# Last pair of an attention stage: the transposed probabilities by halves, and steps of three engines reordered

## The reference, cut to what matters

```
x  = x + xattn(layernorm(x), ctx)
x  = x + ffn(layernorm(x), lists, W1, b1, W2, b2)

xattn(h, c):   n = rmsnorm(h) * norm_w ;  v = concat(n, c)
               a = softmax(mask((n q_w^T)(v k_w^T)^T / 16)) ;  t = a v
               alpha = sigmoid(h gate_w^T + gate_b)
               return (1 - alpha) * h + alpha * t
ffn(x):        for each expert e:  g = x[list_e] ;  y = gelu(g W1_e + b1_e) W2_e + b2_e
               out[list_e] += y * combine_weight_e
```

## Time and profile before

| what | value |
|---|---|
| median of 3 runs (lowest, highest) | 274.86 us (274.32, 274.90) |
| the profiled execution: its own time | 275.01 us |
| its span, first to last instruction | 273.2 us |
| granted TensorE clock | 0.996 of full speed |
| PE busy | 263.7 us (97%) |
| DVE, ACT, POOL busy | 218.4, 188.2, 156.9 us |

### The profile page before, as it was taken

One profiled execution on the slowest core, in us unless ns is written; L12 is line 12 of the kernel. 1 busy time (PEld: TensorE's weight loads), 2 busy tenths in 40 slices (PEclk: granted clock), 3 DMA queues, 4 the chain that ended last, 5 costly groups with the idle time before them and its releaser, 6 DMA issues.

```text
span 273.2 us, 5127 instructions
## 1 busy us (share of the span) xinstructions
PE 263.7 (97%) x1477; PEld 225.8 (83%) x1477; DVE 218.4 (80%) x553; ACT 188.2 (69%) x349; POOL 156.9 (57%) x152
## 2 busy tenths in 40 slices
PE   7899999999989999999999999999999999999993
PEld 3688899999876888888888888888888888888983
DVE  1899999899985779968878896796887889689453
ACT  2687899887666975786676587668657758773540
POOL 4349765565768717656456466655645656514525
PEclk9999999999999999999999999999999999999998
DMA  5986257588446945454464544645446561210211
GB/s 154 341 232 199 94 154 200 148 231 270 133 149 150 388 154 157 129 169 155 134 208 154 156 142 135 168 118 207 160 138 180 160 181 56 59 35 34 65 49 69
DMA packets 30560, 42.44 MB, mean 155 GB/s; under 512 B 5521, under 2 KB 24283, under 8 KB 30416
## 3 DMA queue, kind: packets, MB, share of 16 engines
q1 hardware_dynamic: 25120, 29.74, 35.0%
q0 software_dynamic: 4608, 12.24, 15.4%
q10 hardware_dynamic: 816, 0.26, 0.4%
HBM read 33.54 MB, written 9.24 MB: 157 GB/s over the span
## 4 chain that ended last, share of the span: by engine, by line
PE 81%; DVE 6%; issue 4%; DMA 4%; POOL 1%; ACT 1%; SPq 0%; DVEq 0%; POOLq 0%
PE bank L1423 19%; PE bank L1202 12%; PE bank L1203 12%; PE bank L1204 12%; PE bank L1424 10%; PE bank L1250 4%; PE bank L1294 3%; DMA x_all<-in_x_dram 2%; PE bank L1351 2%; DMA x_all<-token_rows,idx_all 2%; PE bank L1370 1%; PE bank L1371 1%; PE bank L1374 1%; PE bank L1318 1%; POOL out_dram L557 1%
## 5 line engine op out<-in xcount | busy, mean ns | idle before, releaser
L752 ACT ACTIVATE keysT<-bank,biasT 128x512 f32<-128x512 f32 x63 | 43.6, 692 | 55.6 <-PE bank L1204 39.3
L557 POOL DMA_INDIRECT out_dram<-h,sidx x32 | 36.7, 1146 | 40.2 <-DVE h L1094 34.8
L547 POOL DMA_INDIRECT x_all<-out_dram,idx_all x32 | 36.6, 1143 | 23.6 <-DMA out_dram<-h,sidx 16.0
L1202 PE MATMUL bank<-x_hi,w_parts 128*128 128x512 f32 (+1 forms) x114 | 45.1, 396 | 0.0
L1203 PE MATMUL bank<-x_lo,w_parts 128*128 128x512 f32 (+1 forms) x114 | 44.4, 389 | 0.0
L1204 PE MATMUL bank<-x_hi,w_parts 128*128 128x512 f32 (+1 forms) x114 | 44.1, 387 | 0.0
L1119 DVE TENSOR_TENSOR g_lo<-keysT,g_hi 128x512 fp32r<-128x512 f32 x32 | 22.1, 692 | 27.0 <-ACT g_hi L753 26.3
L543 POOL DMA_INDIRECT x_all<-token_rows,idx_all x28 | 30.7, 1095 | 18.9 <-DVE factor L1143 12.4
L1423 PE MATMUL bank<-w_parts,g_hi 128*128 128x512 f32 x112 | 40.5, 396 | 0.0
L1124 DVE TENSOR_TENSOR w_parts<-w_raw,w_parts 128x512 fp32r<-128x512 f32 x56 | 38.4, 686 | 0.0
L758 ACT CAST w_parts<-w_raw 128x512 fp32r<-128x512 f32 x56 | 34.9, 623 | 0.0
(11 more groups left out here) (187 smaller groups left out, 681.5 us busy)
## 6 DMA issues: line engine op xcount, KB each, us to landing
w_raw<-in_L_ffn_W_dram SPq DMA_DIRECT2D x32, 512.0 KB
idx_rows<-in_L_ffn_top_idx_dram SPq DMA_DIRECT2D x8, 256.0 KB, 4.1
out_dram<-x SPq DMA_DIRECT2D x8, 256.0 KB, 2.9
hn_cnat<-in_ctx_dram SPq DMA_DIRECT2D x7, 256.0 KB, 2.8
token_rows<-xn SPq DMA_DIRECT2D x7, 256.0 KB, 2.2
hn_cnat<-in_L_ffn_b_dram SPq DMA_DIRECT2D x1, 1024.0 KB
x_all<-in_x_dram SPq DMA_DIRECT2D x3, 256.0 KB, 6.8
x_all<-in_x_dram SPq DMA_DIRECT2D x1, 768.0 KB, 9.4
```

What stands on the lines that cost most here:

```text
L547: g.indirect_dma_start(accg[:, t, :], None, flat, list_of(e, t)).then_inc(acc_in[t], 16)
L557: g.indirect_dma_start(flat, idx(sidx[:, t:t + 1].bitcast(U32), 0), newrow[:, t, :], None, bounds_check=N - 1, oob_is_err=False).then_inc( ...
L752: a.activation(g32[:, f % NG, :], ps_up[f % 2][:, :], ACT.Gelu_apprx_tanh, bias=bias)
L1202: t_.matmul(dst, lhs_hi, rhs_hi, start=first, stop=False)
```

## The change

In the last pair only: the probabilities of each batch are transposed into a bank of their own, the first batch's between the two halves of the gate products, the second's behind the bias transpose; ACT copies each as it comes, and PE multiplies each by the values as its copy comes. ACT's cast of pair 5's high part moves behind the two copies, PE's products with it behind the values. DVE's subtraction for pair 5's low part moves from before the first mix to behind the second variance. PE's order behind the values becomes: pair 5's high part, tiles 0 and 1, pair 6's high part, tile 2, pair 5's low part, pair 7's first high part, tile 3, pair 6's low part, L1339 and L1342. On POOL, in pair 6, the power of pair 5 (L481) comes ahead of the low part of the weights (L497) instead of behind it.

```diff
--- before.py
+++ after.py
@@ -167,6 +167,8 @@
         ps_gate = banks[5][:, :].rearrange("p (b t) -> p b t", b=2)
         ps_pT = banks[6][:, :].rearrange("p (b j s) -> p b j s", b=2, j=2)
         ps_pv = banks[7][:, :].rearrange("p (b t) -> p b t", b=2)
+        ps_pT_last = [banks[6][:, 0:H].rearrange("p (j s) -> p j s", j=2),
+                      banks[1][:, 0:H].rearrange("p (j s) -> p j s", j=2)]
         ps_pv_last = [banks[7][:, 0:H], banks[4][:, 0:H]]
         ps_list = banks[6]
         ps_up = banks[0:2]
@@ -220,6 +222,8 @@
         exp_rdy = sem("exp_done")
         pT_mm = sem("probs_transposed")
         pT_ev = sem("probsT_ready")
+        last_pT_mm = sem("last_probs_transposed")
+        last_pT_ev = sem("last_probsT_ready")
         gate_mm = sem("gate_product")
         gate_rdy = sem("gate_logit_ready")
         tanh_rdy = sem("tanh_done")
@@ -300,6 +304,9 @@
             body(LAST - 1, 0, 3)
             body(LAST, 1, 3)
 
+        def is_last_but_one(pair):
+            return isinstance(pair, int) and pair == LAST - 1
+
         def has_second_next(pair):
             return not isinstance(pair, int) or pair + 2 < NPAIR
 
@@ -515,9 +522,11 @@
                     x_powers(10, NB, 5)
                     hn_shifts(10, NB, 5)
                 else:
-                    if not is_last(p):
+                    if not is_last(p) and not is_last_but_one(p):
                         expert0_lo(p - 1)
                     rstd(p - 1, 1 - s)
+                    if is_last_but_one(p):
+                        expert0_lo(p - 1)
                 if is_last(p):
                     gather_first_rows(range(NT - 1, NT))
 
@@ -649,10 +658,6 @@
                 a.copy(w_hi[:, 0, col], w_raw[:, col]).then_inc(whi_rdy, 1)
 
             def attention(p, s, use):
-                if is_last(p):
-                    act.wait_ge(xn_rdy, 2 * p - 2)
-                    act.wait_ge(q_mm, NPAIR)
-                    a.copy(late_hi[0], xn2[:, s, :, :]).then_inc(late_hi_rdy, 1)
                 for b in range(2):
                     act.wait_ge(log_rdy, 2 * p + b + 1)
                     a.activation(probs[:, b, :], probs[:, b, :], ACT.Exp, bias=neg_mx[:, b:b + 1], scale=-1.0,
@@ -662,8 +667,16 @@
                     hn_rows(2, 0)
                 elif has_second_next(p):
                     hn_transposed(p + 2, s)
-                act.wait_ge(pT_mm, p + 1)
-                a.copy(probsT, ps_pT).then_inc(pT_ev, 1)
+                if is_last(p):
+                    for b in range(2):
+                        act.wait_ge(last_pT_mm, b + 1)
+                        a.copy(probsT[:, b, :, :], ps_pT_last[b]).then_inc(last_pT_ev, 1)
+                    act.wait_ge(xn_rdy, 2 * p - 2)
+                    act.wait_ge(q_mm, NPAIR)
+                    a.copy(late_hi[0], xn2[:, s, :, :]).then_inc(late_hi_rdy, 1)
+                else:
+                    act.wait_ge(pT_mm, p + 1)
+                    a.copy(probsT, ps_pT).then_inc(pT_ev, 1)
                 if is_first(p):
                     act.wait_ge(hnT_lo_rdy, 2)
                     normed_transposed(1, 1)
@@ -974,11 +987,6 @@
                         h_rows(p + 1, 1 - s)
                 dve.wait_ge(exp_rdy, 2 * p + 2)
                 v.reciprocal(rinv[:, :], rsum[:, :]).then_inc(ri_rdy, 1)
-                if is_last(p):
-                    dve.wait_ge(late_hi_rdy, 1)
-                    dve.wait_ge(xn_rdy, 2 * LAST - 2)
-                    v.tensor_tensor(late_lo[0], xn2[:, s, :, :], late_hi[0].bitcast(F32), ALU.subtract)\
-                        .then_inc(late_lo_rdy, 1)
                 if is_first(p):
                     x_rms(4, 10, 4)
                     dve.wait_ge(x_steps, steps[0])
@@ -1033,6 +1041,10 @@
             last_pair_mixed(1)
             last_pair_shift(0)
             last_pair_variance(1)
+            dve.wait_ge(late_hi_rdy, 1)
+            dve.wait_ge(xn_rdy, 2 * LAST - 2)
+            v.tensor_tensor(late_lo[0], xn2[:, last_s, :, :], late_hi[0].bitcast(F32), ALU.subtract)\
+                .then_inc(late_lo_rdy, 1)
             dve.wait_ge(late_hi_rdy, 2)
             dve.wait_ge(xn_rdy, 2 * LAST)
             v.tensor_tensor(late_lo[1], xn2[:, 1 - last_s, :, :], late_hi[1].bitcast(F32), ALU.subtract)\
@@ -1240,6 +1252,15 @@
                     last = t_.transpose(ps_gate[:, k, o * P:(o + 1) * P], wts[:, 2, o, k * P:(k + 1) * P], ident[:, :])
             last.then_inc(setup_mm, 1)
 
+            def last_probs_transposed(b):
+
+                if b == 0:
+                    pe.wait_ge(pT_ev, NPAIR - 1)
+                pe.wait_ge(exp_rdy, 2 * LAST + b + 1)
+                for j in range(2):
+                    last = t_.transpose(ps_pT_last[b][:, j, :], probs[:, b, j * S:(j + 1) * S], ident[:, :])
+                last.then_inc(last_pT_mm, 1)
+
             def attention(p, s, use):
                 pe.wait_ge(q_ev, p + 1)
                 pe.wait_ge(cT_ev, p + 1)
@@ -1260,6 +1281,8 @@
                     for k in range(KH):
                         last = three_passes(ps_gate[:, b, :], hnT_hi[:, s, k, c], hnT_lo[:, s, k, c],
                                             gateT_hi[:, k, :], gateT_lo[:, k, :], k == 0, k == KH - 1)
+                    if is_last(p) and b == 0:
+                        last_probs_transposed(0)
                 last.then_inc(gate_mm, 1)
                 if has_second_next(p) and not is_first(p):
                     hn_transposes(p + 2, s)
@@ -1269,25 +1292,26 @@
                     pe.wait_ge(bias_in, 16)
                     t_.transpose(banks[0][:, 0:NE * NF], bias_rows[:, :], ident[0:NE * NF, 0:NE * NF])\
                         .then_inc(setup_mm, 1)
-                pe.wait_ge(exp_rdy, 2 * p + 2)
-                for b in range(2):
-                    for j in range(2):
-                        last = t_.transpose(ps_pT[:, b, j, :], probs[:, b, j * S:(j + 1) * S], ident[:, :])
-                last.then_inc(pT_mm, 1)
+                if is_last(p):
+                    last_probs_transposed(1)
+                else:
+                    pe.wait_ge(exp_rdy, 2 * p + 2)
+                    for b in range(2):
+                        for j in range(2):
+                            last = t_.transpose(ps_pT[:, b, j, :], probs[:, b, j * S:(j + 1) * S], ident[:, :])
+                    last.then_inc(pT_mm, 1)
                 if not is_last(p):
                     query(p + 1, 1 - s)
                 if is_first(p):
                     hn_transposes(2, 0)
-                if is_last(p):
-                    pe.wait_ge(log_rdy, 2 * NPAIR - 1)
-                    pe.wait_ge(late_hi_rdy, 1)
-                    for b in range(2):
-                        late_rows(0, b, late_hi, first=b == 0)
-                pe.wait_ge(pT_ev, p + 1)
+                if not is_last(p):
+                    pe.wait_ge(pT_ev, p + 1)
                 pe.wait_ge(n_rdy, p + 1)
                 if not is_first(p):
                     pe.wait_ge(diff_rdy, 2 * p)
                 for b in range(2):
+                    if is_last(p):
+                        pe.wait_ge(last_pT_ev, b + 1)
                     for j in range(2):
                         context = cnat_last if is_last(p) else cnat[:, s, :, :]
                         values = normed[:, s, :, :] if j == 0 else context
@@ -1319,17 +1343,21 @@
                               start=first, stop=False)
 
             each_pair(pe, attention)
-            early_rows(range(1))
+            pe.wait_ge(log_rdy, 2 * NPAIR - 1)
+            pe.wait_ge(late_hi_rdy, 1)
+            for b in range(2):
+                late_rows(0, b, late_hi, first=b == 0)
+            early_rows(range(2))
+            pe.wait_ge(late_hi_rdy, 2)
+            for b in range(2):
+                late_rows(1, b, late_hi)
+            early_rows(range(2, 3))
             pe.wait_ge(late_lo_rdy, 1)
             for b in range(2):
                 late_rows(0, b, late_lo)
-            early_rows(range(1, NT - 1))
-            pe.wait_ge(late_hi_rdy, 2)
-            for b in range(2):
-                late_rows(1, b, late_hi)
-            early_rows(range(NT - 1, NT))
             pe.wait_ge(late_hi_rdy, 3)
             late_rows(2, 0, late_hi)
+            early_rows(range(NT - 1, NT))
             pe.wait_ge(late_lo_rdy, 2)
             for b in range(2):
                 late_rows(1, b, late_lo)
```

## The result

The changed kernel takes 276.18 us (median of 11 runs, 275.77 to 277.94), the kernel before 274.91 (274.12 to 275.29) beside it: ratio 1.0065, 95% interval 1.0048 to 1.0082. The direction is as forecast. The size is larger than forecast: three of the 11 runs lie at 277.66 to 277.94 and form a group of their own, which the forecast does not hold, and the other eight (275.77 to 276.63) lie around 276.1. The median is 0.46% above the one before. The ratio is higher because it weighs the three: the means are 276.60 and 274.79 (1.0066), and 276.15 without the three (1.0050). The profiled execution took 276.63 us (span 274.8), one of the upper ones of the eight.

A forecast was written before the change was run, and what follows sets the result against it. PE was taken to bound the kernel; line 1339, at 81.87, was put at 82.92, a loss of 1.05 us: 275.01 + 1.05 = 276.06, less 0.15 the profiled run lay over the median, 275.9 us; range 275.2 to 276.5.

The forecast's parts named there:

- PE bounds, and what follows passes a shift unshortened: Eight experts, 90 to 260 us: PE busy 170.00 of 170.00 us, so earlier or later starts reach the end whole.
- rival 3: After the last pair: the loss is absorbed later, giving 274.9 us; chance 0.08.
- Root moved, shift held: Pair 5's power (reciprocal root) runs 0.74 us sooner; GpSimd's weight low part holds DVE's shift to 69.84, next difference +0.37.
- Rival 1: Pair 5's shift on DVE is not held up by GpSimd: loss 0.75 us, 275.6 us; chance 0.27.
- Rival 4: GpSimd's power of pair 5 holds DVE as well, some 0.6 us more at the end: 276.5 us; chance 0.05.
- M, and the low products behind it: M, the last pair's first mix on DVE, starts at 75.0 to 75.3; pair 5's low part follows at M + 5.03.
- my bound of 1.5: Upper bound in us of the loss at line 1339: gathers late by 0.37, both half copies at 0.59.
- the gathers may slip by 0 to 0.37: GpSimd's gathers in the last pair may come later by that many us, with pair 5's held shift.
- The sum for PE behind the gather: PE's products from pair 5's low part to line 1339 take 2.77 us; with 4.06 behind pair 6's cast, line 1339 at 82.9.
- rival 2: Last pair: first gather lands 1.5 us sooner, PE has no gap; gain about 0.5 us, 274.4 us; chance 0.10.

The follow-up runs named there:

- tail alone: Kernel before with only PE's new order of tiles, high and low parts, and DVE's low part of pair 5 behind both variances: 275.89 us, ratio 1.0047.
- version with room: Kernel before with pair 5's low products ahead of tile 0 and one weight piece's low part moved from GpSimd to idle VectorE time: 274.46 us, ratio 0.9993.
- the four variants: Changed kernel with the power's move undone (1.0047), pair 5's low part back before the mixes (1.0095), shift before weight low part (1.0081), or PE's gaps made one (1.0109).
- root alone: Kernel before with only GpSimd's power of pair 5 moved ahead of the weight low part: 275.34 us, ratio 1.0020.
- halves alone: Kernel before with probabilities copied by halves and pair 5's cast and high products moved behind copies and values: 274.93 us, ratio 1.0009.

## Why the forecast came out as it did

**PE bounds, and what follows passes a shift unshortened: right.** 170.00 of 170.00 again, and two kernels with the last step 1.48 (changed) and 1.08 us later (tail alone) end later by about as much (1.2 at full clock, and 1.16). For a gain one profile shows a cover: 0.41 us sooner was waited away for expert 1's rows at 95 us, while in the version with room 0.50 us sooner met no wait there. The forecast's rival 3 had looked for a cover for losses, and none was found.

**Root moved, shift held: right, to 0.2 us.** The shift took 1.22 us and ended with GpSimd's L504. The new gap before the first transposes was 0.51 us (forecast 0.7), tanh came 5.63 us behind the logits (forecast 74.3 - 68.62 = 5.68). Rival 1 is refuted: the shift takes 1.22 or 1.23 us in all seven profiles in which the low part of the weights starts beside it, and 0.16 in the seven in which it does not. Rival 4 too: the rows of h (L844, 67.80, 0.74 us for two) ran beside the root unheld. The Trainium skill, page "SBUF — State Buffer", section "SBUF: two separate sides", has the ports locked for the whole instruction of the one that starts first; by the durations here that holds for the addition and the subtraction of GpSimd and not for its root. The root is not untouched in turn: pair 6's took 0.91 to 0.93 us in the five profiles in which VectorE's second operation of the first mix (L1009) had started some 0.1 us ahead of it, and 0.73 to 0.75 in the seven in which that operation started behind it.

**M, and the low products behind it: the place right, the size low.** The first mix came 6.53 us behind the logits (6.52 in a second profile; forecast 6.38, and 6.50 with what I allowed for late gathers). From it the forecast had 5.03 us to the first low product and 2.77 to the last step; measured 80.69 - 75.36 = 5.33 and 83.56 - 80.69 = 2.87. Together 83.35 on the clock of before where I took 82.92: +1.48 from the logits where I had +1.05, at the edge of my bound of 1.5. Three terms make up the missing 0.43. VectorE's low part began 79.94 - 68.83 = 11.11 us behind the logits instead of 6.50 + 4.43 = 10.93: +0.18. The products followed its start by 0.75, where I had 0.60, which was the distance between the starts of two VectorE operations and not the low part's whole length: +0.15. PE's last stretch took 0.10 more. The last two are in the tail-only kernel as well (79.96 - 79.22 = 0.74, and 2.87) and have nothing to do with gathers.

For the first, the term "the gathers may slip by 0 to 0.37" came nearly in full, and I had taken 0.12 of it. The late shift holds back GpSimd's addition of x and h, this holds VectorE's L899 (0.95 us; 0.79 in the kernel with the root put back), and the gathers start 3.17 us behind the logits instead of 2.84. Behind them comes pair 6's root, at 7.15 us instead of 6.81, and it took 0.91 us instead of 0.74. So pair 6's shift is waited for at 76.93, in the midst of the chain that ends in the low part. The slip is not needed for such a wait. With pair 5's root put back the gathers start at 2.84 again and the shift still waits, since the first mix is sooner and pair 6's root takes 0.93:

```profile
74.28 0.48 DVE L1004 SCALAR_TENSOR_TENSOR diff<-bank,rinv,h 128x256 f32<-128x256 f32 x1
74.88 0.93 POOL L488 TENSOR_TENSOR rstd<-var_eps,half_neg 128x2 f32<-128x2 f32 x1
75.84 0.16 DVE L928 SCALAR_TENSOR_TENSOR shift<-mv,rstd 128x2 f32<-128x2 f32 x1 [0.16 <-POOL rstd L488]
78.85 0.69 DVE L1044 TENSOR_TENSOR M_lo<-xn,M_hi 128x512 fp32r<-128x512 f32 x1
```

From the first mix to the low part that is 4.57 us, 4.58 in the changed kernel, and 4.39 in the tail-only kernel, where the shift did not wait.

**The clock: the step that failed.** The sum for PE behind the gather used the durations of the earlier trace rows, all taken at 2.4 GHz. In 7 of 17 runs of the changed kernel the mean granted clock was 0.990 to 0.994, and they came out 1.8 us later (1.1 to 1.9 in the four variants). That the fall stands right behind the new gaps is seen in the three profiles of its variants and not in one of its own. I had counted the new gaps by their length (0.7 us, and the waits ahead of the high and low products) and never asked for the clock behind them. No rival held it, and it is all that lies above 276.63 in the two series of the changed kernel. The first series had three of those in 11, the second four in 6; the measured ratios, 1.0065 and 1.0109, differ by that share. The forecast of 275.9 over 274.86 is a ratio of 1.0038; at full clock the first series has 1.0050. So without the fall the forecast would have been right in kind and some 0.3 us low.

**Not listed either: tile 1.** In the old order it is read behind tile 0 and four products, and in the profile of before its landing did not show. In the new one it is wanted at 76.5, 0.4 us behind tile 0. In seven profiles of this order it was waited for until some time from 76.57 to 78.48, its gather taking 3.4 to 5.4 us from issue to landing. It prolongs the idle stretch more often than it holds what follows: of the five profiles without fills, the cast released pair 6's high products in three, and the tile in two (with the root back they start at 78.58, and the cast had ended at 77.84). Why a landing takes 5 us in one run and 3 in the next I could not settle. Tile 0 shows the reverse: it was read without a wait at 76.13, 4.13 us behind its issue, where it had taken 76.72 - 71.46 = 5.26 before. In all nine profiles with the probabilities by halves it had landed by 4.15 us or sooner. So the condition of rival 2 was half met, tile 0 more than 1 us quicker, and nothing was gained, since the cast and the low part came later.

**How the parts add up.** Tail order alone +1.16, root alone +0.58, halves alone +0.2 (not told apart from nothing): 1.94, where the whole at full clock is 276.1 - 274.7 (the medians of before in the first two series of experiments) = 1.4. That the parts share waits, so that a PE waiting for pair 6's cast hides part of the held shift, would account for it; no run isolates it.

## What to carry to other kernels

Where three engines run level, work that is ready early is worth most where the bounding engine would otherwise wait: the products moved to the back were the filler of its waits. A step moved forward on a helper engine is priced by what starts right behind it, here a subtraction that held a two-column operation for its whole length. When a change adds idle time ahead of dense matrix work, take repeated runs and read the granted clock behind the gap: a loss of 0.5% became one of more than 1% in 7 of 17 runs here.

## What was not expected of the hardware

- After a PE busy for 0.89 us in 76 to 79 the granted clock was 0.69, 0.50, 0.50 and 0.60 in the four windows behind, with PE busy again in them (1.71 us lost). In 20 of 43 runs of the changed kernel and its variants the mean clock was 0.990 to 0.994, in the others 0.996 or more. The Trainium skill's page "TensorE: Matmul & The Clock Gate", section "What's actually happening", says that what the chip watches runs free, so that the same kernel meets it differently from run to run; that 20 of 43 fell agrees, but no run here shows that this is the reason.
- Products of zeros in the gaps (two and five of 128x512 bf16) kept the clock in 11 of 11 runs, without making PE much busier in 76 to 79 (1.09 and 1.33 us in the two profiles, against 1.06 in one that lost it).
- A VectorE operation of two columns takes 1.22 us beside a GpSimd subtraction, 0.16 beside none.
- A GpSimd root of two columns that started 0.1 us behind a VectorE operation of 256 columns took 0.91 us, and 0.73 to 0.75 where it started first.
